# Conditioning rows in column tiles, six sums a head, statistics ahead of masks, banks waited for singly

## The chip, the cores and the metric

The kernel runs on one core of one Trainium2 chip. The metric is the device time of one execution in microseconds (us). Everything is float32; the attention scores use float32r operands (a float32 split into two parts).

## What is computed

Input x is 2 sequences of 2048 rows of 512. A conditioning vector of 1024 a sequence goes through silu and, in each of four layers, through a 1024 x 1024 (layer 0: 1024 x 1536) matrix that gives a scale and a shift (and a gate). Cut to what matters:

```
e = silu(cond) @ W_emb + b_emb;  scale, shift = split(e)          # every layer, [2, 512] each
layer 0: xn = layernorm(x)*(1+scale)+shift; x = x + gate * mamba(xn)     # 1024 channels, 16 states, scan over time
layer 1: q, k, v = layernorm(x) @ Wq, Wk, Wv;  16 heads of 32
         att = softmax(q k^T + (1-mask)*-1e6, over keys);  y = att @ (v*mask)
         x = x + silu(layernorm(y)*(1+scale)+shift) @ Wo + bo
layers 2, 3: q = softmax(q, in a head); k = softmax(k, over time, masked); y = q (k^T v)
         x = x + silu(layernorm(y)*(1+scale)+shift) @ Wo + bo
```

## The kernel before

Six stages run one after the other, each with its own buffers and semaphores; each ends with a barrier of all engines (`Room.close`). Instructions of each engine are written out in order, with semaphore waits by hand.

1. `stage_mamba`: layer 0, in 8 chunks of 512 rows. A chunk is 64 steps (8 channel tiles x 8 pairs of states): ScalarE makes decays, VectorE drives and scans (L617, L627), GpSimd multiplies by C, TensorE sums states. Before the first step come the statistics, the transposes, the conditioning rows (`film_pe`, `film_dve`), the input projection and the convolution taps.
2. `stage_qkv`: layer norm, q, k, v in 8 chunks; q and k go to DRAM in two parts, v stays in the chip. At the end TensorE makes the conditioning rows of layers 1 and 2 (`films`), whose two 4 MB weight tiles ScalarE's queue loads at the start.
3. `stage_attention`: 32 heads (2 sequences x 16). A head has 16 units, one for each tile of 128 keys. In unit u TensorE makes four score matmuls of unit u+1 (`score_mm`, 512 queries each), interleaved with four maximum matmuls of the next head (`max_mm`; VectorE reduces each, L1336), then four value matmuls in four column tiles of 32 (`pv_mm`), and after some units a denominator group. ScalarE makes exponentials into four slots `prob` (`exp`). For the denominators GpSimd adds two units' probabilities in two halves of 128 x 1024 (L1191) into `pair_sum`, and `den_mm` multiplies that by ones in four column tiles, 8 groups a head. In unit 13 the next head's maxima are transposed (`turn_max`), split, and sent by SP into two rows of the q stack (L1163), on which the next head's first score matmul (issued in unit 15) waits; in unit 2 the head before's output is turned (`turn_o`). ScalarE copies the output bank after unit 15 (`copy_o`).
4. `stage_out`: layer 1's second norm, silu, output projection and residual, in 8 blocks of four banks; then the conditioning rows of layer 3 (`film_3`).
5. and 6. `stage_linear`, for layers 2 and 3: norm, k, q, v products, softmaxes, k^T v and output.

The conditioning rows use a 2-column stationary tile and stream 512 columns of weights, 16 products in two halves, then eight transposes of 2 x 128:

```
mm = nc.tensor.matmul(f.ps_row[half][0:NB, :], silu[:, k, :], f.w[:, k, half * D:(half + 1) * D],
                      start=(k == 0), stop=(k == KC - 1))
...
mm = nc.tensor.transpose(f.ps[:, t, :], f.row[:, t * P:(t + 1) * P], f.keep["ident"][0:NB, 0:NB])
```

At the start of stages 2, 5 and 6 VectorE makes its masks first, which wait for small loads, and then the statistics of chunk 0. A float32 matmul shows as two records in the trace.

Of the kernel before, what the change touches and what calls it, by code (L numbers as in the profile page):

```python
# [115 lines left out]

class Film:
# [4 lines left out]
    def __init__(self, r, keep, layer, w, banks):  # L122
# [3 lines left out]
        self.row = r.sb(f"film{layer}_row", [NB, 2 * D])  # L126
# [8 lines left out]

def film_pe(nc, pe, f):
    pe.wait_ge(f.loaded, 16)
    silu = f.keep["silu"]
# [12 lines left out]
def film_dve(nc, dve, f):  # L151
# [3 lines left out]
    for half in range(2):  # L155
        dve.wait_ge(f.row_made, half + 1)
        nc.vector.tensor_copy(f.row[:, half * D:(half + 1) * D], f.ps_row[half][0:NB, :]).then_inc(f.row_copied, 1)
# [17 lines left out]
def stage_mamba(nc, a, keep, bc_dram, out):  # L175
# [4 lines left out]
    with ExitStack() as ctx:  # L180
# [73 lines left out]
                 "cond_in small_in gate_w_in silu_done ident_done neg_done")  # L254
# [326 lines left out]
        def _(dve):  # L581
# [65 lines left out]
            nc.vector.memset(zeros[:, :], 0.0).then_inc(s["zero_done"], 1)  # L647
            norm_stats(0, 0)
# [32 lines left out]
        def _(pe):  # L681
# [103 lines left out]
            pe.wait_ge(s["silu_done"], 1)  # L785
# [132 lines left out]
def stage_qkv(nc, a, keep, src, parts, mask_parts, v, spare):  # L918


    with ExitStack() as ctx:
# [25 lines left out]
        def _(sp):  # L947
# [4 lines left out]

            for b in range(NB):
                each_chunk(sp, b, lambda it: norm_load(sp, m, src, it) if it == 0 else None, chunk)
# [54 lines left out]
        def _(act):  # L1009
# [14 lines left out]

            for b in range(NB):
# [19 lines left out]
                each_chunk(act, b, lambda it: norm(it) if it == 0 else None, chunk)  # L1045

        @block.vector
        def _(dve):
            dve.wait_ge(s["small_in"], 48)
# [4 lines left out]

            def norm(it):
                own = Chain(dve, s["own_dve"], it, DVE_NORM)
                dve.wait_ge(m.x_loaded, (it + 1) * 16)
                norm_dve(nc, dve, m, own, it, lambda t: m.x[:, t, :])
                own.end()
# [13 lines left out]
            for b in range(NB):  # L1073
                each_chunk(dve, b, lambda it: norm(it) if it == 0 else None, chunk)
# [4 lines left out]
def stage_attention(nc, a, keep, parts, mask_parts, v):  # L1079

    with ExitStack() as ctx:
# [7 lines left out]
        PAIRS = QT // 2  # L1089
# [4 lines left out]
        DEN_LAG = 3  # L1094
# [83 lines left out]
        def _(pool):  # L1178
# [5 lines left out]
            for hd in range(HEADS):  # L1184
                for p in range(PAIRS):
                    if hd * PAIRS + p >= 2:
                        pool.wait_ge(s["den_mm"], hd * PAIRS + p - 1)
                    for half in range(2):
                        at = slice(half * HALF, (half + 1) * HALF)
                        pool.wait_ge(s["exp_done"], (hd * QT + 2 * p + 1) * QB + 2 * half + 2)  # L1190
                        nc.gpsimd.tensor_tensor(pair_sum[p % 2][:, at], prob[2 * p % SLOTS][:, at], prob[(2 * p + 1) % SLOTS][:, at],  # L1191
                                                ALU.add).then_inc(s["sum_done"], 1)
                    if p == PAIRS // 2 and hd + 1 < HEADS:
# [3 lines left out]
        def _(pe):  # L1197
# [50 lines left out]
            def den_mm(hd, p):  # L1248

                if p == 0 and hd:  # L1250
                    pe.wait_ge(s["den_read"], hd)
                pe.wait_ge(s["sum_done"], (hd * PAIRS + p + 1) * 2)
# [640 lines left out]
```

## Time and profile before

| what | value |
|---|---|
| median of 3 runs | 5923.78 us (5919.79 to 5928.15) |
| the profiled execution | 5932.34 us |
| its span, first to last instruction | 5930.4 us |
| PE, PEld busy | 5370.3 us (91%), 2515.0 us |
| DVE, ACT, POOL busy | 4102.3 (69%), 2835.2 (48%), 3013.0 us (51%) |
| granted TensorE clock, mean | 0.972 of full |

PE is TensorE's matmuls and PEld its weight loads, DVE is VectorE, ACT ScalarE, POOL GpSimd, SP the engine that only issues transfers; a name with a q (ACTq, SPq) is an engine's queue of issues. L12 is line 12 of the kernel. Busy time of a group is the union of its records, which overlap on PE, so the mean of one can be longer than busy time over count.

In a row the arrow `out<-in` names tiles, then shapes as partitions x elements; `128*32` is a stationary tile of 128 rows and 32 columns. Square brackets hold the engine's idle time before the row and what ended it. The stages lie at about 0 to 2158, 2160 to 2562, 2563 to 4463, 4463 to 4640, 4641 to 5286 and 5287 to 5930 us.

### The profile page before, as it was taken

What the parts mean: (1) busy time and instruction counts of PE and PEld (TensorE: products, weight loads), DVE (VectorE), ACT (ScalarE), POOL (GpSimd) and SP (SyncE); (2) the same over time, 40 slices, a digit from 0 to 9 for tenths busy, and PEclk for the clock granted to TensorE, in tenths of its full rate; (3) what the DMA queues carried; (4) which work ended last, traced back from release to release, by engine and by line L of the source; (5) the groups of instructions that cost most, each with busy time, mean ns of one, the idle gap of its engine ahead of it and who ended that gap; (6) DMA issues with size and microseconds to landing.
All of it is one profiled execution on the core that took longest, in us unless ns stands there. A gap on an engine that the chain in (4) does not pass through costs nothing. (4 is left out here: it accounts for less than half of the span.)

```text
span 5930.4 us, 59426 instructions
## 1 busy us (share of the span) xinstructions
PE 5370.3 (91%) x20064; PEld 2515.0 (42%) x20064; DVE 4102.3 (69%) x5401; ACT 2835.2 (48%) x4895; POOL 3013.0 (51%) x2032
## 2 busy tenths in 40 slices
PE   6888988888898879989999999999998889979898
PEld 2333333333333334434444444444443354544545
DVE  3999999999999952267777777777744445445444
ACT  4757566675756523326565655655661131312121
POOL 4879797887978731126666666666661000000000
PEclk8999999999999989979999999999999999989999
DMA  4020221212121033311011110111103202021101
GB/s 164 22 100 36 95 84 50 77 44 100 61 82 73 27 123 121 111 50 34 23 33 32 24 33 23 33 23 33 34 1 127 85 25 68 16 101 34 59 25 50
DMA packets 116737, 346.32 MB, mean 58 GB/s; under 512 B 12272, under 2 KB 13520, under 8 KB 102032
## 3 DMA queue, kind: packets, MB, share of 16 engines
q1 hardware_dynamic: 96432, 286.07, 14.7%
q0 software_dynamic: 9216, 33.56, 1.5%
q10 hardware_dynamic: 10784, 22.89, 1.0%
q8 instruction: 158, 2.59, 0.2%
q14 instruction: 147, 1.20, 0.1%
HBM read 274.29 MB, written 67.67 MB: 58 GB/s over the span
## 5 line engine op out<-in xcount | busy, mean ns | idle before, releaser
L1336 DVE TENSOR_REDUCE attn_mx<-attn_ps_max 128x1 f32<-128x512 f32 x2048 | 1269.5, 682 | 438.9 <-PE attn_ps_max L1208 434.4
L1191 POOL TENSOR_TENSOR attn_pair_sum<-attn_prob 128x1024 f32<-128x1024 f32 x512 | 1208.5, 2382 | 669.7 <-ACT attn_prob L1302 669.7
L415 POOL TENSOR_TENSOR mamba_hc<-mamba_h,mamba_bc 128x1024 f32<-128x1024 f32 x512 | 1218.2, 2379 | 359.7 <-DVE mamba_h L627 305.9
L1302 ACT ACTIVATE attn_prob<-attn_ps_s 128x512 f32<-128x512 f32 x2048 | 1060.9, 604 | 622.8 <-PE attn_ps_s L1233 619.8
L766 PE MATMUL mamba_y<-mamba_hc,ident 128*128 128x512 f32 x2048 | 1018.4, 621 | 262.9 <-POOL mamba_hc L415 261.1
L521 ACT ACTIVATE mamba_da<-mamba_dt,mamba_a_neg 128x512 f32<-128x512 f32 x1024 | 689.9, 689 | 707.1 <-DVE mamba_h L627 703.2
L627 DVE TENSOR_TENSOR_SCAN mamba_h<-mamba_da,mamba_state,mamba_h 128x512 f32<-128x512 f32 x768 | 939.3, 1264 | 2.1 <-ACT mamba_da L521 1.9
L1233 PE MATMUL attn_ps_s<-attn_q_stack,attn_k_stack 100*128 100x512 f32 x2048 | 861.7, 424 | 11.3 <-DMA attn_q_stack<-attn_m_parts 5.2
L1208 PE MATMUL attn_ps_max<-attn_k_stack,attn_q_stack 98*128 98x512 f32 x2048 | 835.4, 415 | 16.3 <-DMA attn_q_stack<-qk_parts 16.1
L766 PEld LDWEIGHTS mamba_y<-mamba_hc,ident 128*128 128x128 f32 x2048 | 374.1, 194 | 849.8 <-POOL mamba_hc L415 432.7
L617 DVE TENSOR_TENSOR mamba_h<-mamba_du,mamba_bc 128x1024 f32<-128x1024 f32 x512 | 618.6, 1208 | 65.2 <-POOL mamba_state L417 57.1
L1233 PEld LDWEIGHTS attn_ps_s<-attn_q_stack,attn_k_stack 100*128 100x128 f32 x2048 | 387.1, 190 | 464.5 <-issue 181.7
L1244 PE MATMUL attn_ps_o<-attn_prob,attn_v_h 128*32 128x512 f32 x4096 | 545.9, 605 | 0.0
L1208 PEld LDWEIGHTS attn_ps_max<-attn_k_stack,attn_q_stack 98*128 98x128 f32 x2048 | 396.3, 194 | 133.1 <-DVE attn_mx L1336 40.3
L874 POOL TENSOR_TENSOR lin_norm_rstd<-lin_norm_var_eps,neg_half 128x4 f32<-128x4 f32 x16 | 16.1, 1007 | 606.5 <-DVE lin_norm_var_eps L863 606.5
L627 DVE TENSOR_TENSOR_SCAN mamba_h<-mamba_da,mamba_zeros,mamba_h 128x512 f32<-128x512 f32 x256 | 313.2, 1264 | 0.9 <-ACT mamba_da L521 0.8
L874 POOL TENSOR_TENSOR lin_out_norm_rstd<-lin_out_norm_var_eps,neg_half 128x4 f32<-128x4 f32 x16 | 16.1, 1006 | 580.4 <-DVE lin_out_norm_var_eps L863 580.4
L754 PE MATMUL mamba_work<-mamba_w,mamba_zy 128*128 128x512 f32 x512 | 250.3, 615 | 31.6 <-DVE mamba_x_in L645 31.1
L384 POOL TENSOR_TENSOR mamba_u<-mamba_u,mamba_tap 128x512 f32<-128x512 f32 x192 | 251.0, 1309 | 52.8 <-ACT mamba_tap L479 41.8
L1254 PE MATMUL attn_ps_d<-attn_pair_sum,attn_ones 128*32 128x512 f32 x2048 | 266.6, 592 | 1.9 <-POOL attn_pair_sum L1191 1.9
L711 PE MATMUL mamba_work<-mamba_xn_t,mamba_w 128*128 128x512 f32 x512 | 242.9, 601 | 2.4 <-ACT mamba_halo L481 1.4
L722 PE MATMUL mamba_work<-mamba_xn_t,mamba_w 128*128 128x512 f32 x512 | 243.3, 597 | 0.0
(225 smaller groups left out, 5947.8 us busy)
## 6 DMA issues: line engine op xcount, KB each, us to landing
mamba_bc<-bc_dram SPq DMA_DIRECT2D x64, 1024.0 KB, 7.4
mamba_w<-in_in_proj_w_T SPq DMA_DIRECT2D x16, 2048.0 KB, 7.7
qk_parts<-qkv_pair POOLq DMA_DIRECT2D x64, 512.0 KB
attn_k_stack<-qk_parts SPq DMA_DIRECT2D x96, 256.0 KB
attn_q_stack<-qk_parts SPq DMA_DIRECT2D x96, 256.0 KB
mamba_x_in<-in_x SPq DMA_DIRECT2D x16, 1024.0 KB, 6.6
mamba_w<-in_out_proj_w_T SPq DMA_DIRECT2D x8, 2048.0 KB, 8.4
lin_norm_x<-x_after_L SPq DMA_DIRECT2D x16, 1024.0 KB, 5.6
```

The costliest lines, as they stand in the source:

```text
L415: nc.gpsimd.tensor_tensor(hc[:, gs % HC_SLOTS, :, :], h[:, gs % H_SLOTS, :, :], bc[:, g, G:2 * G, :], ALU.mult).then_inc(s["hc_done"], 1)
L521: nc.scalar.activation(da[n % DA_BANKS][:, :], dt[:, ct % 2, :], ACT.Exp, scale=a_neg[:, ct, g * G + j:g * G + j + 1]).then_inc(s["exp_don ...
L617: nc.vector.tensor_tensor(h[:, gs % H_SLOTS, :, :], du[:, :].unsqueeze(1).to_broadcast([P, G, CH]), bc[:, g, 0:G, :], ALU.mult).then_inc(s ...
L627: nc.vector.tensor_tensor_scan(h[:, gs % H_SLOTS, j, :], da[(gs * G + j) % DA_BANKS][:, :], h[:, gs % H_SLOTS, j, :], first, ALU.mult, ALU ...
L766: mm = nc.tensor.matmul(y[ct % 2][:, :], ident[:, :], hc[:, gs % HC_SLOTS, j, :], start=(g == 0 and j == 0), stop=(g == NG - 1 and j == G ...
L1191: nc.gpsimd.tensor_tensor(pair_sum[p % 2][:, at], prob[2 * p % SLOTS][:, at], prob[(2 * p + 1) % SLOTS][:, at], ALU.add).then_inc(s["sum_d ...
L1208: nc.tensor.matmul(free_bank(seq)[:, :], q_st[slot][0:ROWS_MAX, qt * P:(qt + 1) * P], k_st[slot][0:ROWS_MAX, kc * CH:(kc + 1) * CH], start ...
L1233: nc.tensor.matmul(ps_s[n % BANKS][:, :], k_st[slot][0:ROWS, kt * P:(kt + 1) * P], q_st[slot][0:ROWS, c * CH:(c + 1) * CH], start=True, st ...
L1244: mm = nc.tensor.matmul(ps_o[c * DH1:(c + 1) * DH1, :], v_h[hd % 3][:, kt, :], prob[kt % SLOTS][:, c * CH:(c + 1) * CH], start=(kt == 0), ...
L1254: mm = nc.tensor.matmul(ps_d[c * DH1:(c + 1) * DH1, :], ones[:, :], pair_sum[p % 2][:, c * CH:(c + 1) * CH], start=(p == 0), stop=(p == PA ...
L1302: nc.scalar.activation(prob[kt % SLOTS][:, c * CH:(c + 1) * CH], ps_s[n % BANKS][:, :], ACT.Exp).then_inc(s["exp_done"], 1)
L1336: nc.vector.tensor_reduce(mx[hd % 3][:, qt, kc:kc + 1], ps_max[seq % BANKS][:, :], AX.X, ALU.max).then_inc(s["bank_read"], 1)
```

## The change

The conditioning rows: `film_widen` copies silu(cond) 16 times side by side to 32 columns a k-tile; `film_pe` puts four k-tiles in four column tiles of one bank, so a half is two rounds of four products, and the four partial rows are added by a matmul with a 0/1 tile `film_sum` in place of the transpose. In attention the units of a head are summed in six groups of 2 or 3 instead of eight pairs; the sum of a third unit is added to the tile just written. Statistics of chunk 0 come ahead of the masks in three stages, film loads of stage 2 go to SP's queue, the order of weights in `stage_linear` becomes k, q, v, out. In `stage_out` a product waits for its own bank.

```diff
+TILES = 4
+PT = P // TILES
-        self.row = r.sb(f"film{layer}_row", [NB, 2 * D])
+        self.row = r.sb(f"film{layer}_row", [P, 2 * D])
+        self.wide = r.sb(f"film{layer}_wide", [P, KC, PT])
...
+def film_widen(nc, dve, f):
+    nc.vector.tensor_copy(f.wide[:, :, :].rearrange("p k (r b) -> p k r b", b=NB),
+                          f.keep["silu"][:, :, :].unsqueeze(2).to_broadcast([P, KC, PT // NB, NB])).then_inc(f.widened, 1)
 def film_pe(nc, pe, f):
     pe.wait_ge(f.loaded, 16)
+    pe.wait_ge(f.widened, 1)
     for half in range(2):
-        for k in range(KC):
-            mm = nc.tensor.matmul(f.ps_row[half][0:NB, :], silu[:, k, :], f.w[:, k, half * D:(half + 1) * D],
-                                  start=(k == 0), stop=(k == KC - 1))
+        for j in range(KC // TILES):
+            for c in range(TILES):
+                k = j * TILES + c
+                mm = nc.tensor.matmul(f.ps_row[half][c * PT:(c + 1) * PT, :], f.wide[:, k, :],
+                                      f.w[:, k, half * D:(half + 1) * D], start=(j == 0), stop=(j == KC // TILES - 1))
...
-        mm = nc.tensor.transpose(f.ps[:, t, :], f.row[:, t * P:(t + 1) * P], f.keep["ident"][0:NB, 0:NB])
+        mm = nc.tensor.matmul(f.ps[:, t, :], f.row[:, t * P:(t + 1) * P], f.keep["film_sum"][:, :], start=True, stop=True)
...
# stage_mamba, vector, ahead of the first statistics
+            dve.wait_ge(s["ident_done"], 2)
+            nc.vector.tensor_reduce(keep["film_sum"][:, :], ident[:, :].rearrange("p (c r) -> p r c", c=TILES)[:, 0:NB, :],
+                                    AX.X, ALU.add).then_inc(s["sum_set"], 1)
+            dve.wait_ge(s["silu_done"], 1)
+            film_widen(nc, dve, film)
# stage_qkv, sync
+            norm_load(sp, m, src, 0)
+            sp.wait_ge(m.x_loaded, 16)
+            for film in films:
+                film_load(sp, film, a)
# stage_qkv, scalar
-            act.wait_ge(m.x_loaded, 16)
-            for film in films:
-                film_load(act, film, a)
-            act.wait_ge(s["mask_done"], 1)
-            nc.scalar.activation(mrow_parts[:, 0, :], mrow[:, :], ACT.Copy).then_inc(s["mask_done"], 1)
...
+            norm(0)
+            act.wait_ge(s["mask_done"], 1)
+            nc.scalar.activation(mrow_parts[:, 0, :], mrow[:, :], ACT.Copy).then_inc(s["mask_done"], 1)
# stage_qkv, vector: norm(0), film_widen of both films, then the two mask operations (before: the mask operations first)
# stage_attention
-        PAIRS = QT // 2
+        SIZES = (2, 3, 3, 2, 3, 3)
+        GROUPS = [tuple(range(sum(SIZES[:g]), sum(SIZES[:g + 1]))) for g in range(len(SIZES))]
+        NGRP = len(GROUPS)
...
-        DEN_LAG = 3
+        DEN_LAG = 2
...
+                for g, units in enumerate(GROUPS):
+                    if hd * NGRP + g >= 2:
+                        pool.wait_ge(s["den_mm"], hd * NGRP + g - 1)
+                    for n, unit in enumerate(units[1:]):
+                        for half in range(2):
+                            at = slice(half * HALF, (half + 1) * HALF)
+                            pool.wait_ge(s["exp_done"], (hd * QT + unit) * QB + 2 * half + 2)
+                            if n:
+                                pool.wait_ge(s["sum_done"], hd * ADDS + used[units[n], half])
+                            first = pair_sum[g % 2] if n else prob[units[0] % SLOTS]
+                            nc.gpsimd.tensor_tensor(pair_sum[g % 2][:, at], first[:, at], prob[unit % SLOTS][:, at],
+                                                    ALU.add).then_inc(s["sum_done"], 1)
...
-                    if u >= DEN_LAG and (u - DEN_LAG) % 2 == 0:
-                        den_mm(hd, (u - DEN_LAG) // 2)
+                    if u >= DEN_LAG and u - DEN_LAG in GROUP_END:
+                        den_mm(hd, GROUP_END[u - DEN_LAG])
...
# scalar, exp
-                    act.wait_ge(s["sum_done"], (hd * PAIRS + (kt - SLOTS) // 2) * 2 + c // 2 + 1)
+                    before, unit = divmod(hd * QT + kt - SLOTS, QT)
+                    act.wait_ge(s["sum_done"], before * ADDS + used[unit, c // 2])
# stage_out, tensor; its vector queue begins with film_widen(nc, dve, film_3)
-                    pe.wait_ge(s["out_done"], it * TT)
+                    pe.wait_ge(s["out_done"], max(it * TT - TT + t + 1, 0))
# stage_linear
+            pool.wait_ge(s["blocks_set"], 1 + P // dh)
...
-            for i, n in ((0, "Wq"), (2, "Wv"), (1, "Wk"), (3, "Wo")):
+            for i, n in ((1, "Wk"), (0, "Wq"), (2, "Wv"), (3, "Wo")):
                 act.dma_start(w[i][:, :, :], a[names_of[n]].rearrange("(k p) n -> p k n", p=P)).then_inc(w_in[i], 16)
-            act.wait_ge(s["mask_set"], 1)
# scalar: that wait now follows norm(0); vector: small_in, mask and blocks_set waits now follow norm(0)
```

## Rows read from the trace of the kernel before

**Rows 1.** Stretches: busy us (instructions) by engine, PEclk, DMA, GB/s.
```profile
0.00:2160.00 2160.00, 1826.34 (x4040) 732.24 (x4040) 1971.63 (x1819) 1308.28 (x2161) 1690.17 (x1367) 0.97 0.19 70
...
2624.00:4461.00 1837.00, 1823.59 (x10448) 893.66 (x10447) 1267.52 (x2099) 1102.94 (x2143) 1225.66 (x543) 1.00 0.12 27
```

**Rows 2.** Groups by form: busy us, mean ns, idle before, releasers.
```profile
L1336 DVE TENSOR_REDUCE attn_mx<-attn_ps_max 128x1 f32<-128x512 f32 x2048 | 1269.5, 682 | 438.9 <-PE attn_ps_max L1208 434.4
...
L1191 POOL TENSOR_TENSOR attn_pair_sum<-attn_prob 128x1024 f32<-128x1024 f32 x512 | 1208.5, 2382 | 669.7 <-ACT attn_prob L1302 669.7
...
L1233 PE MATMUL attn_ps_s<-attn_q_stack,attn_k_stack 100*128 100x512 f32 x2048 | 861.7, 424 | 11.3 <-DMA attn_q_stack<-attn_m_parts 5.2 <-ACT attn_prob L1302 4.1
```

**Rows 3.** Order of time in attention: start us, us, what.
```profile
3507.03 1.06 PE L1244 MATMUL attn_ps_o<-attn_prob,attn_v_h 128*32 128x512 f32 x8
...
3508.02 0.50 PE L1233 MATMUL attn_ps_s<-attn_q_stack,attn_k_stack 100*128 100x512 f32 x1
...
3510.08 1.06 PE L1244 MATMUL attn_ps_o<-attn_prob,attn_v_h 128*32 128x512 f32 x8
...
3510.96 1.04 PE L1254 MATMUL attn_ps_d<-attn_pair_sum,attn_ones 128*32 128x512 f32 x8
...
3511.93 0.50 PE L1233 MATMUL attn_ps_s<-attn_q_stack,attn_k_stack 100*128 100x512 f32 x1
```

**Rows 4.** Order of time, the last unit of attention.
```profile
4454.74 4.68 POOL L1191 TENSOR_TENSOR attn_pair_sum<-attn_prob 128x1024 f32<-128x1024 f32 x2 [1.38 <-ACT attn_prob L1302]
...
4459.47 1.07 PE L1254 MATMUL attn_ps_d<-attn_pair_sum,attn_ones 128*32 128x512 f32 x8 [1.92 <-POOL attn_pair_sum L1191]
```

**Rows 5.** Order of time, the first conditioning rows.
```profile
25.36 15.98 PE L141 MATMUL mamba_da<-mamba_bc,silu 128*2 128x512 f32 x32
...
34.60 0.68 DVE L157 COPY mamba_film_row<-mamba_da 2x512 f32<-2x512 f32 x1 [23.84 <-PE mamba_da L141]
...
43.32 0.17 DVE L171 TENSOR_TENSOR film<-film,mamba_film_proj 128x8 f32<-128x8 f32 x1
```

**Rows 6.** Order of time after q, k, v, and a group by form.
```profile
2531.20 13.89 PE L141 MATMUL qkv_bank<-spare,silu 128*2 128x512 f32 x32 [0.83 <-issue]
...
2532.78 0.72 POOL L967 DMA_DIRECT2D qk_parts<-qkv_pair  x1 [2.71 <-DVE qkv_pair L1068]
...
2562.07 0.17 DVE L171 TENSOR_TENSOR film<-film,qkv_film_proj 128x8 f32<-128x8 f32 x1
...
L1625 PE MATMUL lin_mm_bank<-lin_kn,lin_v_all 128*128 128x128 f32 x256 | 33.3, 276 | 0.0
```

**Rows 7.** Two stage starts in time, DMA issues (KB, us to landing).
```profile
2162.24 0.71 ACTq L1014 DMA_DIRECT2D qkv_w_v<-in_L_cond_v_w  x1
...
2168.61 0.37 ACTq L133 DMA_DIRECT2D spare<-in_L_cond_emb_w  x1
...
2174.00 2.45 DVE L855 BATCH_NORM_STATS2 qkv_norm_stats<-qkv_norm_x 128x6 f32<-128x512 f32 x4
...
qkv_w_v<-in_L_cond_v_w ACTq DMA_DIRECT2D x1, 1024.0 KB, 9.1
...
4641.13 0.37 SPq L849 DMA_DIRECT2D lin_norm_x<-x_after_L  x1
...
4650.57 2.46 DVE L855 BATCH_NORM_STATS2 lin_norm_stats<-lin_norm_x 128x6 f32<-128x512 f32 x4
...
lin_norm_x<-x_after_L SPq DMA_DIRECT2D x1, 1024.0 KB, 5.9
...
lin_w_k<-in_L_cond_Wk ACTq DMA_DIRECT2D x1, 1024.0 KB, 14.2
```

**Rows 8.** Order of time, the output stage.
```profile
4504.11 0.69 DVE L1464 TENSOR_TENSOR out_x_res<-out_bank,out_x_res 128x512 f32<-128x512 f32 x1 [3.14 <-DMA out_x_res<-x_after_L]
...
4514.88 14.00 PE L1426 MATMUL out_bank<-out_w,out_norm_xn_t 128*128 128x512 f32 x32 [2.03 <-DVE out_x_res L1464]
```

More of the change, by code:

```diff
@@ L156, in film_dve @@
         dve.wait_ge(f.row_made, half + 1)
-        nc.vector.tensor_copy(f.row[:, half * D:(half + 1) * D], f.ps_row[half][0:NB, :]).then_inc(f.row_copied, 1)
+        nc.vector.tensor_copy(f.row[:, half * D:(half + 1) * D], f.ps_row[half][:, :]).then_inc(f.row_copied, 1)
     dve.wait_ge(f.made, 1)
@@ L1059, in norm @@
                 own.end()
+            norm(0)
+            for film in films:
+                film_widen(nc, dve, film)
+            dve.wait_ge(s["small_in"], 48)
+            nc.vector.tensor_scalar(mrow[:, :], mrow[:, :], 1e6, -1e6, ALU.mult, ALU.add).then_inc(s["mask_done"], 1)
+            dve.wait_ge(s["mask_done"], 2)
+            nc.vector.tensor_tensor(mrow_parts[:, 1, :], mrow[:, :], mrow_parts[:, 0, :].bitcast(F32), ALU.subtract).then_inc(s["mask_done"], 1)
             def chunk(it, c, more):
@@ L1088, in stage_attention @@
         LEAD = 3
-        PAIRS = QT // 2
+        SIZES = (2, 3, 3, 2, 3, 3)
+        GROUPS = [tuple(range(sum(SIZES[:g]), sum(SIZES[:g + 1]))) for g in range(len(SIZES))]
+        NGRP = len(GROUPS)
+        GROUP_END = {units[-1]: g for g, units in enumerate(GROUPS)}
+        ADDS = sum(2 * (len(units) - 1) for units in GROUPS)
+        used, sums = {}, {}
+        for g, units in enumerate(GROUPS):
+            for n, unit in enumerate(units[1:]):
+                for half in range(2):
+                    used[unit, half] = 2 * sum(len(x) - 1 for x in GROUPS[:g]) + 2 * n + half + 1
+                    if n == 0:
+                        used[units[0], half] = used[unit, half]
+                    sums[g] = used[unit, half]
         SLOTS = 4
@@ L1184, in _ @@
             for hd in range(HEADS):
[L1185 to L1193, printed above, removed]
+                for g, units in enumerate(GROUPS):
+                    if hd * NGRP + g >= 2:
+                        pool.wait_ge(s["den_mm"], hd * NGRP + g - 1)
+                    for n, unit in enumerate(units[1:]):
+                        for half in range(2):
+                            at = slice(half * HALF, (half + 1) * HALF)
[5 more added lines that the diff above has]
+                                                    ALU.add).then_inc(s["sum_done"], 1)
+                    if g == NGRP // 2 and hd + 1 < HEADS:
                         take_v(hd + 1)
@@ L1246, in pv_mm, with den_mm @@
                 mm.then_inc(s["o_mm"], 1)
[L1248 to L1250 removed]
+            def den_mm(hd, g):
+                if g == 0 and hd:
                     pe.wait_ge(s["den_read"], hd)
[L1252 removed]
+                pe.wait_ge(s["sum_done"], hd * ADDS + sums[g])
                 for c in range(QB):
                     mm = nc.tensor.matmul(ps_d[c * DH1:(c + 1) * DH1, :], ones[:, :],
[L1255 removed]
+                                          pair_sum[g % 2][:, c * CH:(c + 1) * CH], start=(g == 0), stop=(g == NGRP - 1))
                 mm.then_inc(s["den_mm"], 1)
```

40 lines of the change are left out of this document (19 added, 21 removed).

## The prediction

> **What bounds the kernel now.** I read the share of each stage first, then the groups of instructions, then the order of time around each edit. The chain of waits follows only the last stage back to its barrier, so it says nothing of the first five sixths. Every stage ends with a barrier of all engines, so what one stage wins or loses adds to the end, and each can be priced alone.
>
> In attention, 1837 us of the span, TensorE is busy 1823.6 us at the full clock, GpSimd 1225.7, VectorE 1267.5, ScalarE 1102.9 [rows 1]. The reader is to see that only TensorE has no slack. VectorE's row-maximum group sat idle 438.9 us waiting for TensorE, GpSimd's adds 669.7 us waiting for the exponentials; of the score matmuls' 11.3 us of idle time 5.2 are a wait for the DMA of the negated maxima at the turn of a head [rows 2]. In the first stage VectorE is busy 1971.6 of 2160 us [rows 1] in a scan whose order the change leaves alone: what is saved before the scan starts is carried to the end. At the other stage starts TensorE waits for a chain of VectorE, GpSimd and transposes.
>
> **Six sums instead of eight.** A unit (one key tile) is four score and four maximum matmuls, four value matmuls in column tiles, and in every second unit a group of four denominator matmuls. Without the group, from the value matmuls to the next unit's scores is 3508.02 - 3507.03 = 0.99 us, and value to value 3510.08 - 3507.03 = 3.05 us. With it, value to scores is 3511.93 - 3510.08 = 1.85 us. The group costs 1.85 - 0.99 = 0.86 us [rows 3], although its records last 1.04. It goes from 8 to 6 a head, 64 in all: 64 x 0.86 = 55.0 us.
>
> The Trainium skill (TensorEngine Tiling (Array Packing), Key Properties) says that changing the tiling mode drains TensorE. The group stands between value matmuls of its own mode and scores of the full array, so this switch stays whether the group is there or not; the trace agrees, as 0.97 us follow the group and 0.99 the value matmuls. By that rule 0.86 and not 1.04 is the price; with 1.04 the term would be 66.6 us.
>
> What covers the rest: GpSimd has 2 x (1+2+2+1+2+2) = 20 half-width adds a head where it had 16. At 2.382 us [rows 2] that is 47.6 us, with a copy of v of about 0.6 some 48.3. A head takes 1837/32 = 57.4 us [rows 1] and would take about 55.5. Inside a head the tightest stretch is a group of three: four adds, 9.5 us, begin when half of the second unit's exponentials exist. The denominator matmuls come two units after the group's last, some 14 us after that start, since two units without and one with the group are 3 x 3.05 + 0.86 = 10.0 us and the value matmuls of the third come behind. So 4 us are spare, and GpSimd, today idle 669.7/256 = 2.6 us before each pair of adds [rows 2], enters each group without backlog. The new waits (sums for a slot of probabilities, chained adds) lie in order behind adds already done; behind ScalarE's wait would stand the four exponentials of a unit, for which TensorE waits, and behind GpSimd's the next adds alone. The lag constant 2 counts from the last unit and gives the old distance.
>
> The groups now fall after units 3, 6, 9, 11, 14 and 1 of the next head. So unit 14 has one between the maxima's transpose (unit 13) and the next head's first scores, and unit 13 has none. The 0.86 us cover that DMA wait, 5.2 us over the stage [rows 2]: I take 5.0 off. In exchange unit 15 has no group to hide ScalarE's copy of the output bank; the next value matmuls come 3 us later, so it is free; uncovered it would be 0.6 us a head, 19 us.
>
> The last head has no maxima, a shorter unit, and GpSimd is level with TensorE. Today its last two adds (4.68 us) start at 4454.74 and TensorE waits 1.92 us [rows 4]. Four adds now depend on units 14 and 15: 4 x 2.34 = 9.4 us from a start 2.6 us earlier, plus 0.7 us of backlog from the group before: 9.4 - 2.6 + 0.7 - 4.7 = 2.8 us lost. Attention: -55.0 - 5.0 + 2.8 = -57.2 us.
>
> **Conditioning rows in column tiles.** 32 records of 2 x 512 take 13.89 us at the full clock [rows 6]. In tiles, four products of two passes each cost what a denominator or value group costs, 0.88 to 0.97 us [rows 3]; there are four groups, 3.6 us. Against that, eight two-column sums now load 128 x 128 weights in two passes. The nearest row is 256 passes of 128 columns in 33.3 us busy in a group that alternates with others, and its durations of 276 ns overlap [rows 6]: I take 0.11 us from start to start, at most 0.28. Four sums are 0.9 us (2.2 at most) where four transposes took 0.4. The first four hide under the second copy (0.68), the second four do not: +0.5, at most +3.2. The widening copy and the copies of 128 rows instead of 2 are as long per element as before (0.68 for 512 columns [rows 5]) and the first kind is done before the rows' weights land. Per film 13.9 - 3.6 - 0.5 = 9.8 us.
> - After q, k, v: two films from 2531.20 to 2562.2 [rows 6], serial on TensorE: -19.4. The last store of q and k parts is issued at 2532.78 [rows 6] and its transfers end some 4 us later, before the new end at 2543; were it late, a few us would be lost.
> - After the output stage: -9.6.
> - First stage: 15.98 us instead of 13.89 [rows 5], since the clock was at 1.2 GHz for the first 4 us. Of the new 4 groups about 2.4 go slowly (1.76 us each), the others at 0.9: 5.7 us; with the sums the last film operation ends at about 33.9 instead of 43.5: -9.5. Bounds: all slow, -8; none slow, -12.
>
> The Trainium skill (TensorE: Matmul & The Clock Gate, Measured speedup vs the span model) reports 2.38 times for three column tiles, 79% of the ideal. By it four tiles would take 13.89/3.17 = 4.4 us and the four films would give 3.2 us less. The value groups of this trace (four products in 0.88 to 0.97 us, where four untiled ones of this width are 13.89/4 = 3.5) are above 90%, so I stay with the row.
>
> **Statistics ahead of masks.** In the q, k, v stage x has landed by 2168.61, when ScalarE goes on to the film loads; they block its queue, the mask copy comes late, and the statistics start at 2174.00 [rows 7]: -5.3. The film loads move to SP's queue, ahead of the second x load, and now run beside the v, q, k weights instead of behind them. v landed at 2162.24 + 9.1 = 2171.3 [rows 7]; with half the bandwidth from 2168.6 it needs until 2174, with a third until 2177; TensorE will want it at 2178. Free, but with 1 us at the bad end; if it came last, up to 15 us. The second x now lands behind 8 MB near 2199, wanted at 2201.
>
> In each linear stage x lands at 4641.13 + 5.9 = 4647.0 and the statistics wait for the bias rows until 4650.57 [rows 7]: -3.5. k's weights, third in the queue, landed 14.2 us after their issue [rows 7], at about 4658.8 for a first product at 4660.2, which would then be late; they go first in the queue and land near 4653. The mask row waits for q's weights, now second, about 2 us later; its add and the first k tile still precede the third k product. The last stage repeats this: -3.3.
>
> **Banks waited for singly.** TensorE waits 2.03 us before each block's first product for the last residual sum [rows 8]. But VectorE waits 3.14 us for the residual's DMA, which follows the last store, which follows VectorE's own sums: that loop, 18.4 us a block, does not pass through the products. So only the last block's tail gains: -2.0. If the loop did not bind, 6 x 2 = 12.
>
> **Sum.** -9.5 - 5.3 - 19.4 - 57.2 - 2.0 - 9.6 - 3.5 - 3.3 = -109.8 us. The profiled execution took 5932.3 us (span 5930.4 and 1.9 around it): 5822.5. The runs' median is 5923.8, 8.5 lower: 5814.
>
> **Rivals.**
> - *The sums come late* (GpSimd paces part of each head): for it, it becomes the second busiest engine at 87% of a head; against it, the 4 us of slack. If each of the four groups of three cost 0.4 us of waiting, 128 x 0.4 = 51 us: 5865.
> - *The tiles of the rows don't run side by side* (four different weight tiles with four different data): 4 x 10.3 us and the added 2: about 5857. Against it the value matmuls, which do just that.
> - *Weights late in the q, k, v stage*: the 5.3 us and up to 10 more lost, 5819 to 5830.
> - *Slower than before*: a GpSimd add that reads the sum it wrote just before takes longer than one of two probability tiles. At 20a + 0.6 = 57.4 us, a = 2.84 us, GpSimd sets the head; to eat the 52.6 us of the other parts too the head must be 59.0 us, a = 2.92 on average over all 20; as only 8 of 20 are chained, those must take 3.7 us. At 4.0 the head is 12 x 2.38 + 8 x 4.0 + 0.6 = 61.2: 32 x 3.8 - 52.6 = +69, 5993. Nothing in the rows is over 2.4 us for this shape.
> - *More than forecast*: the bank waits bind, the first four value matmuls of a unit lose stalls too: 5800.
>
> **How the numbers follow.** Forecast 0.70, more 0.06, late weights 0.08, late sums 0.10, tiles not parallel 0.04, slower 0.02. The likeliest is 5814. The low end takes the DMA loop as not binding and the first film at its best: 5795; the high end reaches into late sums by half: 5845. A change under 0.2%, 12 us, could not be told from none; that needs nearly all terms to fail: 0.01. Faster 0.97, same 0.01, slower 0.02.
>
> **What would show it.** In the new trace: 1536 records of denominator matmuls instead of 2048 and about 0.86 us less each for 64 groups; value to value still 3.05 us in units without one; GpSimd's adds 640 at 2.38 us; next to no idle time at the turn of a head; film records of about 0.9 us for eight; statistics 5.3, 3.5 and 3.3 us nearer to their stage's start; the output stage's blocks still 18.4 us apart. It would be wrong if TensorE waited for sums in mid-stage, if the add grew, or if a stage start moved its wait to weights.

## The result, and the profile after

| | before | after |
|---|---|---|
| median (lowest to highest), us | 5925.97 (5919.79 to 5929.88), 4 runs | 5819.71 (5813.02 to 5822.55), 4 runs |
| ratio, 95% interval | | 0.9822 (0.981 to 0.9834) |
| profiled execution, its span | 5932.3, 5930.4 | 5820.2, 5818.2 |

The changed kernel is 106 us faster; 5814 was forecast. Each stage ends in a barrier, so the span splits into stages, each counted from its first instruction to that of the next. The table has them for the two kernels and for the four runs of one part alone that are told below:

| stage, us | before | after | sums alone | rows alone | starts alone | banks alone |
|---|---|---|---|---|---|---|
| first | 2160.8 | 2151.3 | 2161.0 | 2151.3 | 2159.3 | 2158.8 |
| q, k, v | 402.6 | 378.7 | 403.3 | 384.5 | 398.0 | 404.0 |
| attention | 1900.5 | 1841.0 | 1840.7 | 1899.7 | 1901.6 | 1901.9 |
| output | 177.2 | 168.9 | 179.0 | 167.0 | 179.6 | 177.6 |
| linear, first | 645.8 | 644.1 | 646.1 | 645.4 | 643.0 | 647.4 |
| linear, second | 643.5 | 634.2 | 638.6 | 638.6 | 637.8 | 641.5 |

The stages that a kernel leaves as they were show the noise of a single profile: up to 2.4 us, and 5 in the last stage (643.5, 638.6, 638.6 and 641.5 for the same code). In the later runs the first linear stage, with the code of the changed kernel, took from 640.2 to 646.6 us, so there a difference of 5 us says nothing either.

The groups by form of the kernel after (busy us, mean ns, idle before, releasers), which answer to [rows 2]:

```profile
L1376 DVE TENSOR_REDUCE attn_mx<-attn_ps_max 128x1 f32<-128x512 f32 x2048 | 1269.5, 682 | 404.7 <-PE attn_ps_max L1247 400.1
...
L1230 POOL TENSOR_TENSOR attn_pair_sum<-attn_prob 128x1024 f32<-128x1024 f32 x384 | 906.5, 2382 | 312.1 <-ACT attn_prob L1342 312.1
...
L1272 PE MATMUL attn_ps_s<-attn_q_stack,attn_k_stack 100*128 100x512 f32 x2048 | 862.3, 424 | 4.2 <-ACT attn_prob L1342 4.2
...
L1230 POOL TENSOR_TENSOR attn_pair_sum<-attn_pair_sum,attn_prob 128x1024 f32<-128x1024 f32 x256 | 604.8, 2387 | 0.0
...
L1293 PE MATMUL attn_ps_d<-attn_pair_sum,attn_ones 128*32 128x512 f32 x1536 | 200.8, 595 | 4.8 <-POOL attn_pair_sum L1230 4.8
...
L903 PE MATMUL out_norm_bank<-ident,out_norm_x 128*128 128x128 f32 x128 | 19.8, 320 | 30.5 <-DVE out_norm_x L885 30.5
...
L1505 DVE TENSOR_TENSOR out_x_res<-out_bank,out_x_res 128x512 f32<-128x512 f32 x32 | 22.1, 692 | 35.2 <-DMA out_x_res<-x_after_L 34.4
```

GpSimd's 512 adds became 384 of two probability tiles and 256 that read the sum just written. The second kind takes 2387 ns against 2382 and never waited. TensorE waited for a sum once in the whole stage, 4.8 us, and the 5.2 us for the DMA of the maxima are gone. The last two lines are the output stage: VectorE still waits for the residual's DMA, 34.4 us over eight blocks, and TensorE's waits now stand ahead of the transposes.

The order of time in attention of the kernel after, a unit without a sum and one with it (start us, us, what), beside [rows 3]:

```profile
3512.82 1.06 PE L1283 MATMUL attn_ps_o<-attn_prob,attn_v_h 128*32 128x512 f32 x8
...
3513.81 0.50 PE L1272 MATMUL attn_ps_s<-attn_q_stack,attn_k_stack 100*128 100x512 f32 x1
...
3515.88 1.07 PE L1283 MATMUL attn_ps_o<-attn_prob,attn_v_h 128*32 128x512 f32 x8
...
3516.76 1.04 PE L1293 MATMUL attn_ps_d<-attn_pair_sum,attn_ones 128*32 128x512 f32 x8
...
3517.73 0.50 PE L1272 MATMUL attn_ps_s<-attn_q_stack,attn_k_stack 100*128 100x512 f32 x1
```

Value matmuls to scores: 0.99 us without, 1.85 with, as before. The price of a sum did not change, only how many there are.

The end of attention, beside [rows 4]:

```profile
4355.87 4.70 POOL L1230 TENSOR_TENSOR attn_pair_sum<-attn_prob 128x1024 f32<-128x1024 f32 x2
...
4360.53 4.63 POOL L1230 TENSOR_TENSOR attn_pair_sum<-attn_pair_sum,attn_prob 128x1024 f32<-128x1024 f32 x2
...
4365.22 1.93 PE L1293 MATMUL attn_ps_d<-attn_pair_sum,attn_ones 128*32 128x512 f32 x8 [4.77 <-POOL attn_pair_sum L1230]
...
4367.08 1.12 PE L1258 MATMUL attn_ps_max<-ident,attn_o_raw 128*128 128x128 f32 x4
```

The last four adds run one behind the other. TensorE waits 4.77 us where it waited 1.92, and then works slowly: 1.93 us for a sum that took 1.07. From the start of that sum to the end of the stage it is 5.8 us where it was 4.4.

The end of the output stage, beside [rows 8], and that stretch by engine (PEclk is the 0.50; columns as in [rows 1]):

```profile
4512.60 3.68 PE L903 MATMUL out_norm_bank<-ident,out_norm_x 128*128 128x128 f32 x16 [4.40 <-DVE out_norm_x L885]
4516.07 14.78 PE L1466 MATMUL out_bank<-out_w,out_norm_xn_t 128*128 128x512 f32 x32
```

```profile
4512.60:4516.00 3.40, 3.40 (x16) 3.40 (x17) 3.30 (x6) 2.09 (x3) 0.00 (x0) 0.50 0.20 77
```

The 2.03 us ahead of the products are gone, and 4.40 us stand ahead of the transposes.

The conditioning rows, after q, k, v and in the first stage, beside [rows 5, 6]:

```profile
2516.93 3.64 PE L154 MATMUL qkv_bank<-spare,qkv_film_wide 128*32 128x512 f32 x32 [0.82 <-issue]
...
2520.50 1.95 PE L160 MATMUL qkv_bank<-film_sum,qkv_film_row 128*128 128x2 f32 x16
2522.38 3.64 PE L154 MATMUL qkv_bank<-spare,qkv_film_wide 128*32 128x512 f32 x32
...
26.19 5.17 PE L154 MATMUL mamba_da<-mamba_bc,mamba_film_wide 128*32 128x512 f32 x32
...
34.02 0.17 DVE L184 TENSOR_TENSOR film<-film,mamba_film_proj 128x8 f32<-128x8 f32 x1
```

The 32 records of a film take 3.64 us instead of 13.89, and from film to film it is 2522.38 - 2516.93 = 5.45 us.

Two stage starts, beside [rows 7]:

```profile
2151.33 0.37 SPq L867 DMA_DIRECT2D qkv_norm_x<-x_after_L  x1
...
2159.39 2.47 DVE L873 BATCH_NORM_STATS2 qkv_norm_stats<-qkv_norm_x 128x6 f32<-128x512 f32 x4 [11.31 <-DMA qkv_norm_x<-x_after_L]
...
4539.89 0.37 SPq L867 DMA_DIRECT2D lin_norm_x<-x_after_L  x1
...
4545.70 2.47 DVE L873 BATCH_NORM_STATS2 lin_norm_stats<-lin_norm_x 128x6 f32<-128x512 f32 x4 [6.85 <-DMA lin_norm_x<-x_after_L]
```

Both now wait for x alone: 8.06 us after the start of the stage where it was 13.22 (2174.00 - 2160.78), and 5.81 where it was 9.44.

### The profile page after: what moved, and what is told of

The parts are those of the page before. It is cut to its first block and busy times, and to the rows that moved or that the text cites. A ratio compares the mean times of both kernels' runs of the same rounds, so it can differ in the third digit from the quotient of the medians.

```text
span 5818.2 us, 58795 instructions
## 1 busy us (share of the span) xinstructions
PE 5255.1 (90%) x19584; PEld 2488.2 (43%) x19584; DVE 4103.5 (71%) x5406; ACT 2832.8 (49%) x4895; POOL 3309.9 (57%) x2160
## 5 line engine op out<-in xcount | busy, mean ns | idle before, releaser
L784 PE MATMUL mamba_y<-mamba_hc,ident 128*128 128x512 f32 x2048 | 995.4, 609 | 275.2 <-POOL mamba_hc L428 273.1
L1230 POOL TENSOR_TENSOR attn_pair_sum<-attn_prob 128x1024 f32<-128x1024 f32 x384 | 906.5, 2382 | 312.1 <-ACT attn_prob L1342 312.1
L1230 POOL TENSOR_TENSOR attn_pair_sum<-attn_pair_sum,attn_prob 128x1024 f32<-128x1024 f32 x256 | 604.8, 2387 | 0.0
L1247 PEld LDWEIGHTS attn_ps_max<-attn_k_stack,attn_q_stack 98*128 98x128 f32 x2048 | 396.7, 194 | 133.0 <-DVE attn_mx L1376 40.3
```

Source lines behind the costliest of these rows:

```text
L784: mm = nc.tensor.matmul(y[ct % 2][:, :], ident[:, :], hc[:, gs % HC_SLOTS, j, :], start=(g == 0 and j == 0), stop=(g == NG - 1 and j == G ...
L1230: nc.gpsimd.tensor_tensor(pair_sum[g % 2][:, at], first[:, at], prob[unit % SLOTS][:, at], ALU.add).then_inc(s["sum_done"], 1)
L1247: nc.tensor.matmul(free_bank(seq)[:, :], q_st[slot][0:ROWS_MAX, qt * P:(qt + 1) * P], k_st[slot][0:ROWS_MAX, kc * CH:(kc + 1) * CH], start ...
```

## The experiments

**One part at a time, on the kernel before.** Six sums in attention:

```
-        PAIRS = QT // 2
+        SIZES = (2, 3, 3, 2, 3, 3)
...
-        DEN_LAG = 3
+        DEN_LAG = 2
```

> The kernel before with one part of the change: six sums per head in attention instead of eight, nothing else. Theory: TensorE sets the head's length and each sum saved is 0.86 us, 64 of them 55.0 us, a head-turn wait gone 5, a later tail +2.8 to +4.6, so -55 to -60 us against before, near 5868 us; the head then takes 55.5 us. Rival, late sums: the chained adds reach TensorE late and the head keeps more of its 57.5 us, -5 to -30 us (5896 to 5921). If the attention stage of the whole change had been helped by another part, this run stays short of -55.

5868.48 us against 5925.99, ratio 0.9896 (0.9881 to 0.9911): -57.5. The whole gain of attention is this edit's (1840.7 us, as in the full change), and the late sums fall.

The conditioning rows alone:

```
+            for c in range(TILES):
+                k = j * TILES + c
-        mm = nc.tensor.transpose(f.ps[:, t, :], f.row[:, t * P:(t + 1) * P], f.keep["ident"][0:NB, 0:NB])
+        mm = nc.tensor.matmul(f.ps[:, t, :], f.row[:, t * P:(t + 1) * P], f.keep["film_sum"][:, :], start=True, stop=True)
```

> The kernel before with the conditioning rows in four column tiles (and the copies and sums that they need), everything else as before. Theory: four such rows lie each wholly on a path (one in the first stage, two at the end of the third, one at the end of the fifth) and each loses 9.5 to 9.7 us, -38.5 us against before, near 5887 us. Rival, tiles not side by side in time: the records keep 0.42 us each, and the change is 0 to +2 us (5926 to 5928).

5887.53 us, ratio 0.9929 (0.9914 to 0.9943): -38.5. By stage: -9.5 in the first, -18.1 after q, k, v, -10.2 after the output.

The stage starts alone:

```
+            norm(0)
             dve.wait_ge(s["small_in"], 48)
...
-            for i, n in ((0, "Wq"), (2, "Wv"), (1, "Wk"), (3, "Wo")):
+            for i, n in ((1, "Wk"), (0, "Wq"), (2, "Wv"), (3, "Wo")):
```

> The kernel before with the starts of three stages alone reordered: statistics of the first block ahead of the masks, film weights issued from SyncE's queue, linear weights loaded in another order. Theory: -5.3 -3.5 -3.3 = -12 us, near 5914 us (-10 to -18 if the last stage's shorter time in the whole change is this part's and not the clock's). Rival, weights late: the reordered loads hold up the first products and the change is 0 to +4 us.

5919.38 us, ratio 0.9987 (0.9977 to 0.9997): -6.6, with an interval from -2 to -14 that holds the 12 forecast. The waits can be read more closely in the trace. The statistics of q, k, v start 7.9 us after the stage's start instead of 13.2. TensorE's wait ahead of the linear transposes, over both stages, in the kernel before and then in this one:

```profile
L885 PE MATMUL lin_turn_bank<-ident,lin_norm_x 128*128 128x128 f32 x224 | 30.3, 294 | 40.3 <-DVE lin_norm_x L867 40.3
```

```profile
L885 PE MATMUL lin_turn_bank<-ident,lin_norm_x 128*128 128x128 f32 x224 | 30.3, 294 | 33.6 <-DVE lin_norm_x L867 33.6
```

That is 6.7 us less where 3.5 + 3.3 were forecast. With the 5.3 of q, k, v it makes 12. The profiled span is 11.1 shorter, of which 1.5 lie in the first stage, whose code is unchanged. The waits went as said; the median cannot tell 6.6 from 12.

The banks alone:

```
-                    pe.wait_ge(s["out_done"], it * TT)
+                    pe.wait_ge(s["out_done"], max(it * TT - TT + t + 1, 0))
```

> The kernel before with one edit: in the output stage TensorE waits for each PSUM bank singly. Theory: the loop over a block is closed by the residual tile (store, next load, add), so TensorE idles as much as before, only in another place: -2 to +2 us, 5924 to 5928 us, and no shorter period of a block. Rival: the wait for the four banks was on the path, each of the eight blocks gives 1.5 us back, -12 us (5914).

5925.40 us, ratio 0.9997 (0.9987 to 1.0006): -0.6 us, with an interval from -8 to +4 that excludes the rival's 12 and not the 2.0 of the prediction. The end of the output stage in the kernel before and in this one:

```profile
4604.57 1.97 PE L885 MATMUL out_norm_bank<-ident,out_norm_x 128*128 128x128 f32 x16 [0.21 <-DVE out_norm_x L867]
...
4608.56 14.00 PE L1426 MATMUL out_bank<-out_w,out_norm_xn_t 128*128 128x512 f32 x32 [2.02 <-DVE out_x_res L1464]
```

```profile
4606.28 2.44 PE L885 MATMUL out_norm_bank<-ident,out_norm_x 128*128 128x128 f32 x16 [2.82 <-DVE out_norm_x L867]
4608.52 15.15 PE L1426 MATMUL out_bank<-out_w,out_norm_xn_t 128*128 128x512 f32 x32
```

Two short waits, 0.21 and 2.02, became one of 2.82 ahead of the transposes. Over the blocks behind the first, TensorE is idle for 13.0 us in the kernel before and 13.3 in this one: it waits as long, in other places. The last block's products took 15.15 us instead of 14.00, with a granted clock of 0.65 in 4608.70 to 4612.00. That is not this edit's doing alone, for the kernel before has such a block too, with the old waits, and the changed kernel has one that waits 2.73 us in one piece and stays fast:

```profile
4547.72 1.97 PE L885 MATMUL out_norm_bank<-ident,out_norm_x 128*128 128x128 f32 x16 [0.44 <-DVE out_norm_x L867]
4551.72 15.70 PE L1426 MATMUL out_bank<-out_w,out_norm_xn_t 128*128 128x512 f32 x32 [2.03 <-DVE out_x_res L1464]
```

```profile
4436.93 1.97 PE L903 MATMUL out_norm_bank<-ident,out_norm_x 128*128 128x128 f32 x16 [2.73 <-DVE out_norm_x L885]
4438.74 13.90 PE L1466 MATMUL out_bank<-out_w,out_norm_xn_t 128*128 128x512 f32 x32
```

**What closes the loop of the output stage.** Two residual tiles in the changed kernel, then the same with the old wait for all four banks:

```
-        x_res = r.sb("x_res", [P, 4, D])
+        x_res = [r.sb(f"x_res{i}", [P, 4, D]) for i in range(2)]
...
+                if it + 1 < NCH:
+                    sp.wait_ge(s["stored"], it * 16 * TT)
+                    residual(it + 1)
```

> The changed kernel with two residual tiles in the output stage, the next block's residual loaded while the block before is stored, nothing else. Theory: the loop store, load, add closed each block at 18.15 us, TensorE's own work in a block is 14.0 of products and 2.0 of transposes, 16.0 us: seven periods shorter by 2.1 us, -15 us against the changed kernel, near 5805 us (-8 if the statistics on VectorE then end last). Rival: the loop is not what binds, the adds on VectorE are: 0 to -3 us.

> The kernel of the run before this one (two residual tiles) with the old wait: TensorE waits for all four banks ahead of each block. Theory: the last block's adds end 1.5 us after its last product, while TensorE does 2.0 us of transposes, so the wait is covered once the residual tile is out of the way: 0 to +2 us against two tiles with single waits. Rival: the single waits are worth what the prediction's other case gave them, 1.5 us in each block, +8 to +12 us.

5795.61 us, ratio 0.978 (0.9765 to 0.9794), and 5795.80, the same ratio: 24 us below the changed kernel for the tiles, 0.2 us for the bank waits. The order of time on TensorE in the kernel with two tiles and single waits:

```profile
4446.12 1.91 PE L903 MATMUL out_norm_bank<-ident,out_norm_x 128*128 128x128 f32 x16
4447.87 13.90 PE L1471 MATMUL out_bank<-out_w,out_norm_xn_t 128*128 128x512 f32 x32
...
4461.60 1.91 PE L903 MATMUL out_norm_bank<-ident,out_norm_x 128*128 128x128 f32 x16
```

and in the one with two tiles and the old wait:

```profile
4448.04 1.91 PE L903 MATMUL out_norm_bank<-ident,out_norm_x 128*128 128x128 f32 x16
4449.78 13.93 PE L1471 MATMUL out_bank<-out_w,out_norm_xn_t 128*128 128x512 f32 x32
...
4463.55 1.91 PE L903 MATMUL out_norm_bank<-ident,out_norm_x 128*128 128x128 f32 x16
```

No line has a wait, and the granted clock stays at 1.00 behind the first block: 15.48 and 15.51 us a block, where the changed kernel's average is 18.3 ((4512.60 - 4384.68) / 7). Seven periods give 127.9 - 110.6 = 17.3 us. The last block gives 2.6 more, as it ran slowly before (3.68 + 14.78 us, now 1.91 + 13.90). The stage is 148.98 us, 19.9 less; the other 4 us of the median lie in stages that the edit does not touch, within their noise. So the residual tile was the loop, and the single waits show no gain with the second tile or without it.

**How far the sums can go.** Fewer sums in the changed kernel:

```
-        SIZES = (2, 3, 3, 2, 3, 3)
+        SIZES = (3, 3, 3, 3, 4)
```

> The changed kernel with five sums per head (groups of 3, 3, 3, 3 and 4 score tiles) instead of six, nothing else. Theory: TensorE still sets the head (55.5 us), GpSimd needs 22 adds of 2.39 us and a copy, 53.1 us, and fits; each sum fewer is worth 0.86 us, 32 of them -27.5 us against the changed kernel, near 5792 us. Rival: with 53.1 us in a head of 54.7 GpSimd comes late at the group of four and a part of it, 0.3 to 0.9 us a head, is given back: -0 to -18 us (5802 to 5820).

5800.35 us, ratio 0.979 (0.9775 to 0.9804): -19, between the two theories. Attention lost 15.4 us (1825.65). TensorE waited for a sum only in the last head:

```profile
4338.58 9.25 POOL L1230 TENSOR_TENSOR attn_pair_sum<-attn_pair_sum,attn_prob 128x1024 f32<-128x1024 f32 x4
...
4347.89 1.93 PE L1293 MATMUL attn_ps_d<-attn_pair_sum,attn_ones 128*32 128x512 f32 x8 [9.00 <-POOL attn_pair_sum L1230]
```

4.2 us went there. A head, from one transpose of the maxima to the next, was 55.03 us in the mean of 31 where 55.63 - 0.86 = 54.77 was due, 8 us over the stage: its first score product waits for the DMA of the maxima again, 0.07 to 0.7 us in nearly every head, where it never does in the changed kernel. The placing was then tried: `SIZES = (3, 3, 3, 4, 3)`.

> Five sums per head again, but with the group of four fourth and not last (3, 3, 3, 4, 3), so that a sum stands in the unit behind the head turn as in the changed kernel. In the run with the group of four last the attention stage lost 15.4 us against the changed kernel where 27.5 were expected: the last sum of the stage was waited for 9.0 us (4.8 in the changed kernel), and the first score product behind a head turn stood 0.14 to 0.3 us longer for the row of maxima in each head. Theory: with the sum back in that unit both go, and the stage is 27 us shorter than the changed kernel's (-24 to -28; near 5793 us). Rival, GpSimd: 22 adds in a head of 54.7 us make TensorE wait wherever the group of four stands: no better than the run with it last (5800).

5794.50 us, ratio 0.9774 (0.9757 to 0.979): 28 below the changed kernel by the ratios. Attention takes 1819.0 us, 22.0 less than in the changed kernel, and a head 54.82 in the mean, with one such wait left. That is better than with the group of four last by 6.6 us, but short of 27: TensorE waits 7.4 us for the last two sums, so the tail did not go back to 4.8. The head's share is shown, the tail's half of the theory was wrong.

Four sums, `SIZES = (4, 4, 4, 4)`:

> The changed kernel with four sums per head (groups of four score tiles), nothing else. Theory: GpSimd now needs 24 adds of 2.39 us and a copy, 57.9 us a head, more than the 53.8 us of TensorE, and sets the head: 57.9 - 55.5 = 2.4 us more than with six sums, +77 us against the changed kernel, near 5896 us, with TensorE idle before the sums. Rival: GpSimd's work stays hidden, -0.86 x 64 = -55 us (5765).

5862.57 us, ratio 0.9892 (0.9876 to 0.9909): +43. TensorE waits for sums in 92 places, 74.1 us together. GpSimd sets the head, as two stretches say (after, then this kernel; columns as in [rows 1]):

```profile
2610.00:4370.00 1760.00, 1749.97 (x9860) 868.74 (x9858) 1256.50 (x2082) 1088.81 (x2123) 1511.33 (x667) 1.00 0.12 27
```

```profile
2610.00:4400.00 1790.00, 1714.30 (x9325) 840.88 (x9323) 1254.43 (x2076) 1086.19 (x2118) 1790.00 (x791) 1.00 0.12 27
```

GpSimd is busy in all of 1790 us. A head is 56.64 us in the mean of 31, not 57.9: adds back to back follow each other every 2.34 us (their mean distance in this trace; 4360.53 - 4355.87 = 4.66 for two in the tail above), and 24 x 2.34 + 0.6 = 56.8. The mean of a record, 2.39, is too long for such a sum. The heads give 31 us of the 43 and the tail behind the last transpose 12.

**The start that the change left.** The same order in the output stage:

```
-            dve.wait_ge(s["weights_in"], 32)
             for b in range(NB):
...
+                if b == 0:
+                    norm(0)
+                    dve.wait_ge(s["weights_in"], 32)
```

> The changed kernel with one edit in the output stage, the one start that the change did not touch: VectorE's wait for the weights and the bias moved behind the first block's statistics. Theory: VectorE stood 7.06 us for the bias that it needs only after the first products; the statistics start 7.0 us earlier and everything behind them too, since the weights have landed by then: -6 to -7 us against the changed kernel, near 5813 us. Rival: TensorE waits for the weights instead, whose landing the statistics only covered: 0 to -2 us.

5816.25 us, ratio 0.9812 (0.9798 to 0.9827). Against the changed kernel that is -3.5 by the medians and -6 by the ratios, which the runs cannot tell from none. The stage is 167.34 us, 1.5 less. The trace shows what came next:

```profile
4371.56 0.43 SPq L139 DMA_DIRECT2D out_film_w<-in_L_cond_W_emb  x1
4372.03 0.96 SPq L1445 DMA_DIRECT2D out_x_res<-x_after_L  x1
...
4377.90 3.68 PE L903 MATMUL out_norm_bank<-ident,out_norm_x 128*128 128x128 f32 x16 [9.32 <-DMA out_bias<-in_L_cond_out_b]
...
4390.79 0.69 DVE L1504 TENSOR_TENSOR out_x_res<-out_bank,out_x_res 128x512 f32<-128x512 f32 x1 [4.60 <-DMA out_x_res<-x_after_L]
```

The transposes start 7.35 us after the stage where it was 13.65, 6.3 of the 7.0 forecast. But the first residual tile is issued behind 4 MB of conditioning weights and is used 18.8 us after its issue. VectorE waits 4.60 us for it, and the statistics of the next block stand behind that add. The rival was right in a small part: TensorE's first transposes wait for the bias and not for the statistics.

**All together**, the five sums, the two tiles and the start, and in the last head a single tile that TensorE sums itself:

```
+        LAST_SIZES = (3, 3, 3, 3, 3, 1)
...
+                if len(units) > 1:
+                    pe.wait_ge(s["sum_done"], hd * ADDS + plans[hd].sums[g])
+                    operand = pair_sum[(hd * NGRP + g) % 2]
+                else:
+                    operand = prob[units[0] % SLOTS]
```

> The changed kernel with five sums per head (3, 3, 3, 4, 3), in the last head groups of 3, 3, 3, 3, 3 and 1 (the last score tile is summed by TensorE directly, without GpSimd), two residual tiles in the output stage and its statistics ahead of the weights. Theory, terms against the changed kernel: five sums -27, the tail of the attention stage -4 (a sum more, 0.9, against a wait of 4.8), residual tiles -20 to -24, start -7: -58 to -62, near 5760 us. Rival: the gains share waits (the tail and the start, or the clock behind a longer idle), and less than 45 is left (over 5775 us).

5768.65 us, ratio 0.973 (0.9716 to 0.9745): 51 below the changed kernel, between the theories. The first residual tile was waited for 3.90 us, the last three-tile sum 4.40 us. Then the queue was put right, TensorE's wait for the weights moved behind the first transposes, and the last groups cut smaller:

```
-            film_load(sp, film_3, a)
...
+                if it == 0:
+                    film_load(sp, film_3, a)
...
-        LAST_SIZES = (3, 3, 3, 3, 3, 1)
+        LAST_SIZES = (3, 3, 3, 3, 2, 1, 1)
```

> The combination of the run before with three edits more: the conditioning weights of the output stage (4 MB, 16.6 us to landing) issued behind the first two residual tiles, TensorE's wait for the weights behind the first block's transposes, and in the last head groups of 3, 3, 3, 3, 2, 1 and 1. In the combination the first residual tile stood behind those 4 MB on the same queue and was waited for 3.90 us, the first transposes waited 1.1 us for the bias, and the last three-tile sum was waited for 4.40 us. Theory: the residual wait goes (-3.9; also in the run that moved the statistics alone it was this that took the gain), the transposes -1.1, the tail -4.4 + 0.9: -8.5 us, near 5760 us. Rival: the gain at the start was lost to something else than the queue (the clock behind a longer idle, the weights themselves), and only the tail's -3.5 shows: 5765 us or more.

5761.60 us, ratio 0.9717 (0.9701 to 0.9734). That is 7.0 below the run before, 58 below the changed kernel, and the fastest of all. By stages attention gave 5.6 us (1814.4 to 1808.8) where 3.5 was expected and the output stage 2.7 (144.9 to 142.2) where 5.0 was; the three edits were not run singly, and the medians alone do not part 5760 from the rival's 5765. Its tail and the start of its output stage:

```profile
4329.07 1.07 PE L1304 MATMUL attn_ps_d<-attn_pair_sum,attn_ones 128*32 128x512 f32 x8
4329.96 1.90 PE L1304 MATMUL attn_ps_d<-attn_prob,attn_ones 128*32 128x512 f32 x16
...
4341.65 3.68 PE L903 MATMUL out_norm_bank<-ident,out_norm_x 128*128 128x128 f32 x16 [8.42 <-DVE out_norm_x L885]
```

No wait for a sum is left, attention is 1808.8 us, VectorE waits for no residual tile, and the output stage is 142.2 us: 6.8 less than with two tiles alone (149.0), which is what the earlier start was to give.

## Why the prediction was right

The method held: each stage priced alone from rows around its edit. Singly the four parts gave -57.5, -38.5, -6.6 and -0.6, -103 in sum, beside -106 together. The forecast had -57.2, -38.5, -12.1 and -2.0.

- **Six sums, -55.0 for 64 of them.** Right, 0.86 us each. Five sums nearly say it again: the mean head goes from 55.63 to 54.82. Taking the distance between neighbours and not the record's 1.04 us made the term 55 and not 67. The distances agree with the rule of the Trainium skill (TensorEngine Tiling (Array Packing), Key Properties) as the prediction used it: 0.99 us to the scores without the group and 0.97 behind it, in both traces. What a switch itself costs no run separates.
- **The cover for the DMA wait, -5.0.** Right in kind, but too small. The 5.2 us of the row are seven waits, of 0.47 to 1.12 us. The trace has 24 more of 0.07 to 0.10, 2 us together, which are too short for the row to count. All are gone in the changed kernel. The mean of 31 heads fell from 57.59 to 55.63 us, by 1.96, and two sums are 1.72 of that: 0.24 a head is left, 7.5 us over the stage.
- **The tail, +2.8.** The wait grew by 2.85 us. Not in the sum was what followed: the granted clock is 0.50 in the 3 us behind it (4365.20 to 4368.20), the 1.2 GHz level, where the kernel before has 1.00 (4459 to 4463), and the rest of the stage takes 1.4 us more. Together +4.2. With the cover at 7.5 attention comes to -55.0 - 7.5 + 4.2 = -58.3 us, beside -59.5 measured.
- **Rows in four column tiles, 3.6 us and 0.9 for eight sum records.** Right: 3.64, and 1.95 for sixteen. Between films 9.55 us are saved where 9.8 was put. The 2.38 times for three tiles of the Trainium skill (TensorE: Matmul & The Clock Gate, Measured speedup vs the span model) would have made it 4.4 us, by the prediction's estimate; four tiles gave 13.89/3.64 = 3.8 times, and the measurement decides.
- **Starts, -5.3 -3.5 -3.3.** The waits fell by 5.2 (q, k, v) and 6.4 (both linear stages, 40.3 to 33.9). The weights were not late. The last stage's 9.3 us less is not all this: unchanged code varies there by 5 us between profiles.
- **Banks, -2.0.** The step that failed, though its mechanism is the right one. The loop through the residual's DMA closes a block, as argued; but "only the last block's tail gains" forgot that the loop reaches the tail too: the last block's transposes stand behind its statistics, and those behind a sum that waits for the residual. The wait moved ahead of the transposes, 4.40 us in one piece. Behind it the granted clock is 0.50 (4512.60 to 4516.00), the transposes took 3.68 us instead of 1.97 and the products 14.78 instead of 14.00. The output stage gained 8.4 us where 11.6 was forecast, with 9.6 for the film in it. How much of the 3.2 us is the edit's and how much a block that happened to run slowly stays open: with the banks alone the wait was 2.82 us, and why it is 4.40 here no run shows. The prediction also took one row for all: TensorE waits 2.02 or 2.03 us before the products in five of the eight blocks of the kernel before, 0.98 in one and not at all in two, and the blocks there are 16.0 to 20.2 us apart and not all 18.4.

By stages the forecast had -9.5, -24.7, -57.2, -11.6, -3.5 and -3.3, -109.8 in sum; the two profiled spans have -9.5, -23.9, -59.5, -8.4, -1.7 and -9.3, -112.2. That the sums are so close is partly luck: attention gained 2.3 us more than forecast and the last stage 6.0, which is near its noise, while the output stage gained 3.2 less, the first linear stage 1.8 and q, k, v 0.8. The 5.7 us between 5814 and 5819.7 are within the spread of single executions (5919.8 to 5929.9 for the kernel before) and need no further term.

## What to carry to other kernels

Price an edit from the distance between neighbours in order of time, not from the length of a record: 0.86 against 1.04 for a group of matmuls, 2.34 against 2.39 for adds back to back. Before a wait is loosened, follow the loop that closes a block: here store, load and add of one tile held it, a second tile took 20 us off its stage and the loosened wait nothing that shows. When a start is moved forward, look through the queue for what is asked for next: a 1 MB tile behind 4 MB of weights that are needed at the end left 1.5 us of the 6.3 by which the transposes began earlier. Before a wait is priced from the total of a row, look how it is spread and whether the shortest ones are counted: the cover for the DMA wait was worth 7.5 us and not 5.2.

## What the runs showed of the hardware

- The granted clock of TensorE fell behind some waits and not behind others of the same length. In the output stage of the kernel before, waits of 0.40 and 2.02 us around a block's transposes left its products at 14.00 us, and 0.44 and 2.03 in the next block gave 15.70, with a granted clock of 0.57 in 4552 to 4556. In the changed kernel one wait of 2.73 us left the products at 13.90, and one of 2.70 gave 2.70 us for the transposes and 14.89 for the products. Behind the wait of the last block (4.40 us there, 4.32, 4.19 and 3.96 in the two runs of five sums and the run of the earlier output start) the transposes took 3.39 to 3.68 us each time. With two residual tiles no wait is left behind the first block, and every later block keeps the clock at 1.00. Why one wait of 2 to 3 us is followed by the lower level and another is not stays open; it was not tried by itself.
- Products of two columns took as long as the loads of their 128 columns of weights: sixteen records in 1.95 us, 0.12 each; in the q, k, v stage 32 such loads are busy 3.7 us and their products 3.9.
- GpSimd adds that read the sum just written run as fast as the others (2387 against 2382 ns), also for three in a chain (2390 with five sums).
